# Scaling of two layer norms moved from VectorE to ScalarE in the last stage of a decoder layer

## The reference, cut to what matters

```python
def _layernorm(x, eps=1e-05):
    return (x - mean(x)) / sqrt(var(x) + eps)
x = x + self_attention(_layernorm(x))          # 16 heads of 32, causal
x = x + cross_attention(_layernorm(x), ctx)    # 16 heads of 128, 64 keys
x = x + experts(_layernorm(x))                 # gate: argmax over 8 experts of rank 64
```

## Time and profile before

| | before |
|---|---|
| median of the runs | 1533.86 us |
| the profiled execution | 1535.35 us |
| its span, first to last instruction | 1533.6 us |
| busy: PE | 1382.5 us (90%) |
| busy: DVE | 1092.7 us (71%) |
| busy: POOL | 757.2 us (49%) |
| busy: ACT | 729.9 us (48%) |
| mean granted TensorE clock | 0.966 |

### The profile page before, as it was taken

The page is one execution under the profiler, slowest core; times in us unless marked ns, Lnnn a source line. Parts: engine busy times, 40 slices in busy tenths (PEclk is TensorE's granted clock), DMA queues, the critical chain, the costliest instruction groups (busy, mean ns, idle before and its releaser), DMA issues.

```text
span 1533.6 us, 28325 instructions
## 1 busy us (share of the span) xinstructions
PE 1382.5 (90%) x10592; PEld 1140.9 (74%) x10592; DVE 1092.7 (71%) x2037; ACT 729.9 (48%) x1739; POOL 757.2 (49%) x570
## 2 busy tenths in 40 slices
PE   7878778999998999999995778999999999999998
PEld 5656667777787877777874567888888887888886
DVE  4336486777878787877775577878787877787865
ACT  5444567666676667676674432323232323232221
POOL 2321266767777676867675643334343433343310
PEclk9999989999999999999998789999999999999999
DMA  8999587879898979888888731313130313030000
GB/s 321 306 316 292 118 153 135 166 159 160 169 162 160 164 141 182 162 168 168 155 145 232 189 144 47 116 34 125 30 138 28 133 33 132 28 136 30 28 15 28
DMA packets 378872, 212.57 MB, mean 139 GB/s; under 512 B 337648, under 2 KB 337776, under 8 KB 375024
## 3 DMA queue, kind: packets, MB, share of 16 engines
q1 hardware_dynamic: 378736, 210.74, 57.1%
HBM read 76.49 MB, written 50.33 MB: 83 GB/s over the span
## 4 chain that ended last, share of the span: by engine, by line
PE 48%; DVE 26%; issue 5%; ACT 4%; DMA 4%; POOL 2%; SPq 0%; DVEq 0%; ACTq 0%; POOLq 0%
PE banks L44 35%; DVE a_neg_max L803 4%; PE banks L936 4%; PE banks L1535 3%; DMA a_turned<-shared 3%; DVE b_xn L1378 2%; PE banks L970 2%; DVE a_y_sum L822 2%; DVE shared L812 2%; ACT a_probs L706 2%; PE banks L944 2%; DVE b_probs L1427 1%; PE banks L971 1%; DVE b_row_sum L1432 1%; DVE b_row_max L1425 1%
## 5 line engine op out<-in xcount | busy, mean ns | idle before, releaser
L626 POOL TENSOR_TENSOR shared<-a_probs,shared 128x768 f16<-128x768 f32 (+1 forms) x192 | 349.4, 1820 | 204.9 <-DVE shared L812 183.0
L706 ACT ACTIVATE a_probs<-banks,a_neg_max 128x128 f32<-128x128 f32 (+3 forms) x512 | 265.1, 531 | 210.9 <-DVE a_neg_max L803 184.0
L803 DVE TENSOR_REDUCE a_neg_max<-banks 128x2 f32<-128x256 f32 (+3 forms) x256 | 203.7, 818 | 115.4 <-PE banks L944 114.7
L1231 POOL TENSOR_TENSOR b_probs<-b_probs,b_row_scale 128x1024 f32<-128x1024 f32 x32 | 61.0, 1907 | 200.8 <-DVE b_row_scale L1437 200.8
L970 PE MATMUL banks<-a_v,a_turned 128*128 128x96 bf16 x1280 | 123.5, 212 | 32.3 <-DMA a_turned<-shared 25.8
L970 PEld LDWEIGHTS banks<-a_v,a_turned 128*128 128x128 f16 x1280 | 99.8, 100 | 65.5 <-issue 34.5
L1212 POOL TENSOR_TENSOR b_rstd<-b_var,b_minus_half 128x1 f32<-128x1 f32 x64 | 35.3, 551 | 189.4 <-DVE b_var L1373 189.4
L1304 ACT ACTIVATE b_probs<-b_probs 128x1024 f32<-128x1024 f32 x32 | 33.9, 1059 | 182.2 <-DVE b_probs L1427 182.2
L971 PE MATMUL banks<-a_v,a_turned 128*128 128x64 bf16 x1280 | 119.3, 196 | 0.0
L44 PE MATMUL banks<-a_xt_hi,w_qkv_hi 128*128 128x512 f32 x256 | 110.5, 432 | 6.5 <-DVE a_yt_lo L777 4.7
L706 ACT ACTIVATION_READ_ACCUMULATOR a_probs<-banks,a_neg_max 128x1 f32 x512 | 105.9, 207 | 0.0
(11 more groups left out here) (172 smaller groups left out, 3983.2 us busy)
## 6 DMA issues: line engine op xcount, KB each, us to landing
m_dram<-c_m_out SPq DMA_DIRECT2D x8, 2048.0 KB, 13.7
vw_dram<-shared SPq DMA_DIRECT2D x32, 512.0 KB, 8.3
b_vw_raw<-vw_dram SPq DMA_DIRECT2D x8, 2048.0 KB, 8.0
shared<-m_dram SPq DMA_DIRECT2D x7, 2048.0 KB, 8.4
c_w_raw<-w_group_dram SPq DMA_DIRECT2D x7, 1280.0 KB, 11.5
a_x_res<-x_dram SPq DMA_DIRECT2D x32, 256.0 KB, 3.5
x_dram<-a_x_res SPq DMA_DIRECT2D x32, 256.0 KB, 2.9
b_x<-x_dram SPq DMA_DIRECT2D x32, 256.0 KB, 2.7
```

The costliest lines, as they stand in the source:

```text
L626: nc.gpsimd.tensor_tensor(part(u, 1), probs[:, u % PROB_SLOTS, 0:2 * columns_of(u // 2)], part(u, 0), ALU.subtract).then_inc(parts_ready, 1)
L706: ins = nc.scalar.activation(probs[:, u % PROB_SLOTS, to:to + width], score[:, j, at:at + width], ACT.Exp, bias=neg_max[:, c:c + 1], accum ...
L803: ins = nc.vector.tensor_reduce(neg_max[:, c:c + 2], score[:, 2 * half:2 * half + 2, at:at + width], AX, ALU.max, negate=True)
L1231: nc.gpsimd.tensor_tensor(probs[:, :, :], probs[:, :, :], row_scale[:, :].unsqueeze(2).to_broadcast([P, XH, S]), ALU.mult).then_inc(probs_ ...
```

## The change

Both `normalise` move from VectorE to ScalarE: as an activation Identity with a scale (the reciprocal deviation) and a bias per row. The bias is the negated mean times the reciprocal deviation. VectorE writes the negated mean (one more 1-column instruction in `layernorm_moments`, ahead of var), and GpSimd multiplies it behind its pow, after a wait for that pow. ScalarE has the scalings behind xt2_hi, ahead of the vw_hi copies 1 and 2. In the run-up it has them at the places that the diff shows. The diff without the declarations:

```diff
@@ -1209,7 +1211,11 @@
     def gpsimd(pool):
         def deviation(k, n):
             pool.wait_ge(var_ready[k], n + 1)
+            if not is_first(n):
+                pool.wait_ge(xn_ready[k], n)
             nc.gpsimd.tensor_tensor(ln[k][3][:, :], ln[k][2][:, :], minus_half[:, :], ALU.pow).then_inc(rstd_ready[k], 1)
+            pool.wait_ge(rstd_ready[k], n + 1)
+            nc.gpsimd.tensor_tensor(ln[k][6][:, :], ln[k][5][:, :], ln[k][3][:, :], ALU.mult).then_inc(shift_ready[k], 1)
         def m_low(b, c, par):
             pool.wait_ge(m_hi_ready, b * CHUNKS + c + 1)
@@ -1299,12 +1305,17 @@
         def flat(ap):
             return ap[:, :, :].rearrange("p k w -> p (k w)")
+        def normalise(k, src, n):
+            _, _, _, rstd, xn, _, shift = ln[k]
+            act.wait_ge(shift_ready[k], n + 1)
+            nc.scalar.activation(xn[:, :], src, ACT.Identity, bias=shift[:, :], scale=rstd[:, :]).then_inc(xn_ready[k], 1)
+
         def exponentials(n):
             act.wait_ge(shifted, n + 1)
             nc.scalar.activation(probs[:, :, :], probs[:, :, :], ACT.Exp).then_inc(exp_ready, 1)
         def step(b, t, par):
-            done, gated, made_tile, ahead = (neighbour(b, t, d) for d in (-1, -2, -3, 1))
+            done, gated, made_tile, ahead, far = (neighbour(b, t, d) for d in (-1, -2, -3, 1, 2))
             here = b * TT + t if is_tile(b) else None
             second = is_second(here)
             new_vw = t == 0 and is_tile(b)
@@ -1332,6 +1343,10 @@
                 copy_hi(flat(ht_hi), turn[1][:, :], ht_full, made_tile[2] + 1, ht_hi_ready)
             if ahead:
                 copy_hi(flat(xt2_hi), turn[0][:, :], xt2_full, ahead[2] + 1, xt2_hi_ready)
+            if far:
+                normalise(2, x1[:, far[1], :], far[2])
+            if done:
+                normalise(3, x2[:, done[1], :], done[2])
             if new_vw:
                 split_vw(b, 1)
                 split_vw(b, 2)
@@ -1342,14 +1357,17 @@
             if new_vw:
                 split_vw(b, 3)
+        normalise(2, x1[:, 0, :], 0)
         act.wait_ge(m_first_loaded, 16)
         for c in range(CHUNKS):
             split_m(0, c, 0)
         yield
         copy_hi(flat(xt2_hi), turn[0][:, :], xt2_full, 1, xt2_hi_ready)
+        normalise(2, x1[:, 1, :], 1)
         for c in range(CHUNKS):
             split_vw(0, c)
         copy_hi(flat(xt2_hi), turn[0][:, :], xt2_full, 2, xt2_hi_ready)
+        normalise(2, x1[:, 2, :], 2)
         exponentials(0)
         yield
         run(act, step)
@@ -1364,18 +1382,16 @@
         def layernorm_moments(k, src, n):
-            stats, moments, var, _, _ = ln[k]
+            stats, moments, var, _, _, minus_mean, _ = ln[k]
             nc.vector.bn_stats(stats[:, :], src).then_inc(stats_ready[k], 1)
             dve.wait_ge(stats_ready[k], n + 1)
             nc.vector.memset(beat[:, :], 0.0).then_inc(moments_ready[k], 1)
             nc.vector.bn_aggr(moments[:, :], stats[:, :]).then_inc(moments_ready[k], 1)
             dve.wait_ge(moments_ready[k], 2 * (n + 1))
+            if not is_first(n):
+                dve.wait_ge(shift_ready[k], n)
+            nc.vector.tensor_scalar(minus_mean[:, :], moments[:, 0:1], -1.0, None, ALU.mult)
             nc.vector.tensor_scalar(var[:, :], moments[:, 1:2], EPS, None, ALU.add).then_inc(var_ready[k], 1)
-
-        def normalise(k, src, n):
-            _, moments, _, rstd, xn = ln[k]
-            dve.wait_ge(rstd_ready[k], n + 1)
-            nc.vector.tensor_scalar(xn[:, :], src, moments[:, 0:1], rstd[:, :], ALU.subtract, ALU.mult).then_inc(xn_ready[k], 1)
         def layernorm2_moments(tile):
             b, t, n = tile
@@ -1471,10 +1487,6 @@
                 low(flat(ht_lo), turn[1][:, :], flat(ht_hi), ht_hi_ready, made_tile[2] + 1, ht_ready)
             if ahead:
                 low(flat(xt2_lo), turn[0][:, :], flat(xt2_hi), xt2_hi_ready, ahead[2] + 1, xt2_ready)
-            if far:
-                normalise(2, x1[:, far[1], :], far[2])
-            if done:
-                normalise(3, x2[:, done[1], :], done[2])
             if t == 0 and here is not None:
                 vw_low(b, VW_DVE[0])
             if second:
@@ -1502,14 +1514,12 @@
         nc.vector.tensor_reduce(any_key[:, :], mask_f[:, :].rearrange("p (b s) -> p b s", b=B), AX, ALU.max).then_inc(consts_ready, 1)
         layernorm2_moments((0, 0, 0))
         yield
-        normalise(2, x1[:, 0, :], 0)
         yield
         m_low(1)
         m_low(3)
         yield
         low(flat(xt2_lo), turn[0][:, :], flat(xt2_hi), xt2_hi_ready, 1, xt2_ready)
         layernorm2_moments((0, 1, 1))
-        normalise(2, x1[:, 1, :], 1)
         yield
         for c in VW_DVE:
             vw_low(0, c)
@@ -1521,7 +1531,6 @@
         shift(0)
         layernorm2_moments((0, 2, 2))
         scale_of_rows(0, 0)
-        normalise(2, x1[:, 2, :], 2)
         yield
         probs_low(0)
         yield
```

More of the change, by code:

```diff
@@ L1072, in cross_attention_and_experts @@
     ln = {k: (sb(f"stats{k}", [P, 6], F32), sb(f"moments{k}", [P, 2], F32), sb(f"var{k}", [P, 1], F32),
-              sb(f"rstd{k}", [P, 1], F32), at(f"xn{k}", PLACE[f"xn{k}"], [P, D], F32)) for k in (2, 3)}
+              sb(f"rstd{k}", [P, 1], F32), at(f"xn{k}", PLACE[f"xn{k}"], [P, D], F32),
+              sb(f"minus_mean{k}", [P, 1], F32), sb(f"shift{k}", [P, 1], F32)) for k in (2, 3)}
     row_max = sb("row_max", [P, XH], F32)
@@ L1110, in cross_attention_and_experts @@
     rstd_ready = {k: sem(f"rstd{k}_ready") for k in (2, 3)}
+    shift_ready = {k: sem(f"shift{k}_ready") for k in (2, 3)}
     xn_ready = {k: sem(f"xn{k}_ready") for k in (2, 3)}
```

## The result

The changed kernel takes 1551.16 us (median of 4 runs, 1546.75 to 1551.8) against 1533.66 (4 runs, 1531.5 to 1535.66) before: ratio 1.0101, interval [1.0081, 1.012]. It is slower by 17.5 us where 8.4 were forecast. The profiled execution took 1550.72 (span 1548.9), 15.4 more than the one before. (The three stages in the description of the kernel before are: products of the cross attention's weights and the context, the self attention, the cross attention with the experts.)

A forecast was written before the change was run, and what follows sets the result against it. TensorE sets the pace, so only its gaps can be won. Six batches 7.1, seventh 0.9, last steps 0.1 and run-up 0.3 sum to +8.4 us, forecast 1542.3 us; range 1525 to 1548, the forecast case's own 1537 to 1549.

The forecast's parts named there:

- the working: Step t=0 timed instruction by instruction: the 1.38 us xn gap goes, but held gate instructions start hidden 0.75 later.
- The scaling on ScalarE: Each norm's scaling on ScalarE: 0.81 us, between ends of 0.62 and 1.0.
- The multiplication: GpSimd's new 128x1 multiplication behind its pow, per norm: 0.3 us, plus 0.05 for the wait.
- the end of the shift: VectorE's shift by the row maximum at t=1, unable to pass GpSimd's m_low: 1.12 us later.
- the sum: Loss per loop batch: shift 1.12 us later plus 0.07 for the third norm at ht_lo, 1.19 us.
- the ht_lo wait at t=1: TensorE's product late in t=1 that waited 0.77 us for ht_lo would start 1.19 us later.
- both rivals: At t=0, both gate instructions slip past GpSimd (1519.6 us, chance 0.16), or only one is held (1527.2 us, chance 0.20).
- At t=2 and t=3 TensorE is the limit again, so nothing is made good and nothing more is lost: Later steps of each batch: no recovery and no further loss beyond the 1.19 us.
- six batches: The six loop batches of the last stage at 1.19 us each: 7.1 us lost.
- the run-up: Work up to t=2 of the first batch: +0.3 us, between -3.1 and +3.5.
- behind the loop: Seventh batch, which has no m_low, 0.9 us, and last steps 0.1 us.
- its range: The forecast case's own range of execution time, 1537 to 1549 us, from low and high ends of its terms.

The follow-up runs named there:

- e2: Changed kernel plus 14 transposes on TensorE, results unread, during the ht_lo wait at t=1 of every batch: 1544.51 us, ratio 1.0058.
- e4: Kernel before plus two unused reductions on VectorE ahead of ht_lo at t=1 of every batch: 1546.94 us, ratio 1.0064.
- e11: Changed kernel with GpSimd's m_low at t=1 held until VectorE's shift by the row maximum: 1541.16 us, ratio 1.0041.
- e3: Changed kernel with ScalarE's vw_hi copies 1 and 2 ahead of both scalings at t=0: 1547.73 us, ratio 1.0067.
- e6: Changed kernel with the second norm's scaling back on VectorE, only the third norm's on ScalarE: 1541.84 us, ratio 1.0038.
- e7: Changed kernel with only GpSimd's last vw_low at t=0 held until gate_one is done: 1532.71 us, ratio 0.998.
- e10: Kernel before with one wait: GpSimd's first vw_low at t=0 comes after the third norm's xn; 1531.89 us, ratio 0.998.
- e9: Kernel before, GpSimd waiting three times: first vw_low behind third norm's xn, second behind gate_one, m_low at t=1 behind VectorE's shift; 1519.62 us, ratio 0.9891.

## Why the prediction missed

**Right, step by step.** GpSimd's last pow at t=0 starts 5.78 later on the clock of this trace than before (1210.81 against 1205.03). With 5.78 taken off, against the working: VectorE's vw_low starts at 1207.69 (1207.8) and ends at 1209.30 (1209.45); gate_rank ends at 1211.59 (1211.7), gate_one at 1213.95 (1214.1), pt_lo at 1216.54 (1216.65), and TensorE begins the attended product at 1216.67 (1216.7). The scaling on ScalarE takes 0.815 (median of 64; 0.81 worked out), minus_mean 0.154. The multiplication takes 0.19 (I took 0.3), and the end of the shift moved by 0.94 instead of 1.12. In the first loop batch TensorE's gaps of over 0.06 us come to 3.37 instead of 2.19: 1.18, where the sum had 1.19; the batch itself grew by 1.31. That the two agree to 0.01 is partly luck: the ht_lo wait at t=1 grew by 0.99 (0.75 to 1.74) and not by 1.19, and small waits at t=2 and at the next t=0 (0.14 and 0.06 longer), which the sum had at nothing, make up the rest.

Two instructions of 8 columns were held too: 1.52 and 2.13 us against 0.23. The trace thus agrees with the lock by GpSimd that the Trainium skill describes (page SBUF — State Buffer, section Who interferes with whom). The two times rule out both rivals, which let one or both slip past.

**The step that failed** is "At t=2 and t=3 TensorE is the limit again, so nothing is made good and nothing more is lost". More is lost: the granted clock, 1.00 throughout the loop before, falls behind the longer ht_lo wait, and the matmuls behind it run slower for a while. I priced a longer gap as the gap alone. In the change this costs 8.0 us over the loop (e2), in five of its six batches, as much again as the hold itself; e4 brings it about in the kernel before, and e2 and e11 take it away with the gate chain still held.

**The sum again**, on the profiled executions (spans, 15.3): six batches 15.65 against 7.1, of which 8.0 the clock and the rest 1.28 a batch; the run-up -1.0 against +0.3, by TensorE's timelines at t=2 of the first batch, before and in the change:

```profile
931.86 1.97 PE L1535 MATMUL banks<-ident,b_probs 128*128 128x128 f32 x8 [7.01 <-DVE b_xt_lo L1360]
...
930.82 1.97 PE L1544 MATMUL banks<-ident,b_probs 128*128 128x128 f32 x8 [6.58 <-DVE b_xt_lo L1378]
```

and about 0.7 against 1.0 behind the loop. The run-up thus worked the other way by 1.3; ScalarE's first exponentials came 3.4 later (884.39), not 6.6, and by t=2 that was made good. The medians lie 2.1 further apart than the profiled pair, since the profiled run of before was 1.7 above its median and that of the change 0.4 below. From the prediction's own terms its range is 1536.4 to 1549.6, not 1537 to 1549.

**What stays open**: why the clock didn't fall in the first batch behind the same wait (1.74 us there, in the change, and 1.81 in e4), and why e3 kept it in three batches of six. Waits of 1.37 to 1.64 in e6, e7 and e10 were not followed by a fall in any loop batch. Every fall in the loop came behind an ht_lo wait of 1.73 or more, but waits of 1.71 to 1.81 also passed without one, so its length alone does not decide. How often the clock fell in executions without a profile is not shown.

## What to carry to other kernels

Taking one instruction off VectorE, because GpSimd holds it, does not free the instructions queued behind it: ask which instruction now stands beside GpSimd's long one, and whether it is on the path. An order does more than a move here: three waits for GpSimd in the kernel before (e9) give a ratio of 0.9891, without the change. And a wait added to a TensorE that has run at full clock can have two prices: its length, and slower matmuls behind it when the granted clock falls (8.0 us beside 7.65 here); read PEclk in windows of a few us behind the longest gaps.

## What the runs showed of the hardware

An 8-column VectorE instruction took 2.13 us beside 128x1024 GpSimd subtractions instead of 0.23 (the change; 2.15 in e10), nearly as long as a held 512-column scaling (4.75 for two, before). In the change a TensorE wait of 1.76 us was followed by 12 matmuls that took 4.61 us instead of 3.04, so that the wait cost 1.57 more than its length. With 14 transposes inside that wait (e2) the granted clock stayed at 1.00.
